# Gated delta stage: the decayed state enters the update banks by identity products, and ScalarE copies it back

## The reference, cut to what matters

```python
q = causal_dwconv_silu(x @ Wq.T, qcw, qcb).reshape(B, T, H, DK)
k = causal_dwconv_silu(x @ Wk.T, kcw, kcb).reshape(B, T, H, DK) * SCALE
v = causal_dwconv_silu(x @ Wv.T, vcw, vcb).reshape(B, T, H, DV)
a = sigmoid(x @ Wa.T + ba).reshape(B, T, H, DV)
beta = sigmoid(x @ Wb.T + bb)
def step(S, inp):                       # one token, all batches and heads
    qt, kt, vt, at, bt = inp
    err = einsum('bhij,bhj->bhi', S, kt) - vt
    S = at[..., None] * S - bt[..., None, None] * (err[..., None] * kt[:, :, None, :])
    return S, einsum('bhij,bhj->bhi', S, qt)
_, o = lax.scan(step, S0, xs)
o = (o - mean(o)) / sqrt(var(o) + EPS) * ln_w + ln_b      # over one head's 64 channels
o = (o * sigmoid(x @ Wg.T).reshape(B, T, H, DV)) @ Wo.T
```

## Time and profile before

| what | value |
| --- | --- |
| time before, median of 3 runs | 2882.89 us (2877.66 to 2885.38) |
| the profiled execution | 2865.99 us, span 2864.2 us |
| PE busy in the span | 2368.0 us, 83% |
| DVE busy in the span | 2144.6 us, 75% |
| ACT busy in the span | 1545.3 us, 54% |
| the gated delta stage | from about 53 to 1300 us of the span |

### The profile page before, as it was taken

One profiled execution on the slowest core, in us unless ns is written; L12 is line 12 of the kernel. 1 busy time (PEld: TensorE's weight loads), 2 busy tenths in 40 slices (PEclk: granted clock), 3 DMA queues, 4 the chain that ended last, 5 costly groups with the idle time before them and its releaser, 6 DMA issues. The chain is left out here.

```text
span 2864.2 us, 63246 instructions
## 1 busy us (share of the span) xinstructions
PE 2368.0 (83%) x25445; PEld 1633.2 (57%) x25445; DVE 2144.6 (75%) x4003; ACT 1545.3 (54%) x3976; POOL 264.0 (9%) x278
## 2 busy tenths in 40 slices
PE   6778778777777887787993999999997886999777
PEld 5677667666666777774441666666642232232376
DVE  6999999999999999993114677778726785886465
ACT  3555566666555555564233677777641113667344
POOL 0000000000000000000011101110002342110342
PEclk9788887888887787878996999999998998999889
DMA  5110111110111111102005999999500002230421
GB/s 184 32 31 18 31 31 32 32 32 17 31 32 32 32 24 24 31 17 71 1 11 151 230 248 227 237 240 233 137 32 11 0 1 86 59 98 24 170 71 64
DMA packets 205723, 219.44 MB, mean 77 GB/s; under 512 B 32966, under 2 KB 191446, under 8 KB 199990
## 3 DMA queue, kind: packets, MB, share of 16 engines
q1 hardware_dynamic: 203033, 210.44, 28.1%
q0 software_dynamic: 2400, 4.95, 0.5%
HBM read 137.96 MB, written 79.79 MB: 76 GB/s over the span
## 5 line engine op out<-in xcount | busy, mean ns | idle before, releaser
L2809 DVE TENSOR_REDUCE dl_ZO<-dl_XP 128x64 f32<-128x128 f32 (+6 forms) x448 | 219.7, 490 | 15.4
L2805 DVE TENSOR_TENSOR dl_XP<-dl_ZO,dl_G 128x64 f32<-128x64 f32 (+6 forms) x448 | 194.6, 434 | 15.4
L1990 ACT ACTIVATE da_AB<-ps 128x384 f32<-128x384 f32 x256 | 124.7, 491 | 142.4 <-PE ps L1851 138.7
L2143 DVE TENSOR_TENSOR ps<-ps,da_window 128x192 f32<-128x192 f32 (+1 forms) x256 | 101.3, 396 | 118.1 <-PE ps L1874 113.8
L1470 DVE TENSOR_REDUCE ra_top<-ps 128x1 f32<-128x512 f32 x256 | 159.2, 680 | 36.2 <-PE ps L1236 35.3
L2000 ACT ACTIVATE da_E<-ps,da_top 128x512 f32<-128x512 f32 x256 | 176.2, 688 | 17.4 <-DVE da_top L2146 16.9
L2146 DVE TENSOR_REDUCE da_top<-ps 128x1 f32<-128x512 f32 x256 | 176.9, 691 | 8.8
L1881 PE MATMUL ps<-ident,da_E 128*128 128x128 f32 x1024 | 168.8, 288 | 1.3 <-ACT da_E L2000 1.2
L1370 ACT ACTIVATE ra_PT<-ps 128x512 f32<-128x512 f32 x256 | 136.0, 601 | 61.0 <-PE ps L1267 60.7
L2380 PE MATMUL ps<-X,dl_taps_q 128*128 128x128 f32 x1088 | 149.7, 305 | 1.2 <-DVE dl_taps_q L2870 1.2
L2380 PEld LDWEIGHTS ps<-X,dl_taps_q 128*128 128x128 f32 x1088 | 146.5, 221 | 3.3 <-DVE dl_taps_q L2870 1.4
(11 more groups left out here) (408 smaller groups left out, 5760.5 us busy)
## 6 DMA issues: line engine op xcount, KB each, us to landing
da_bands<-da_AB SPq DMA_DIRECT2D x128, 384.0 KB, 3.8
dl_Abc<-dl_ends SPq DMA_DIRECT2D x64, 512.0 KB, 6.3
da_window<-da_bands SPq DMA_DIRECT2D x128, 192.0 KB, 4.3
da_across<-da_bands SPq DMA_DIRECT2D x128, 192.0 KB, 4.4
da_parts<-da_split SPq DMA_DIRECT2D x64, 96.0 KB, 3.4
ra_parts<-ra_split SPq DMA_DIRECT2D x16, 384.0 KB, 3.7
rf_We<-in_rf_We SPq DMA_DIRECT2D x1, 4608.0 KB, 23.3
da_K<-da_parts SPq DMA_DIRECT2D x16, 256.0 KB
```

The lines of the kernel that those rows point to most:

```text
L1990: eng.activation(AB[:, j % STAGES, h, :, :], ps[:, band_bank(v), 0:2 * BAND].rearrange("p (k x) -> p k x", k=2), ACT.Copy)\
L2805: link(eng.tensor_tensor(XP[:, :, :, SB - t:], seen.unsqueeze(1).to_broadcast([P, 2, I, t + 1]), G[:, x:x + 2, keys][:, ::-1, :].unsqueeze ...
L2809: link(eng.tensor_reduce(ZO[:, to:to + 1 + (2 * I - 1) * CH:CH].rearrange("p (k i) -> p k i", k=2), XP[:, :, :, SB - 1 - t:], AXX, ALU.add))
```

## The change

1. `end` on VectorE no longer adds. In `boundary` TensorE multiplies the identity with the decayed state's quarter into each update bank (`kept`), and the update products add to it. In the first half all four quarters are put in ahead of the wait for `W`; in the second half three, and the fourth comes after the updates of the first three, because its bank 1 is used for the transposes there. ScalarE copies each bank back to the state (`keep_state`), between the decays' copy (now `lay_decays`) and the rest of `lay_out`. VectorE waits for these copies before it decays the state again.
2. The transposes of `boundary` go to banks 2 and 3 in the first half and to bank 1 in the second, and the keys across to banks 2 and 3. TensorE's wait for the key copies moves behind the first two projections. The seventh projection moves ahead of the second `middle`.
3. The values are transposed into the buffer of the beta weights instead of `Y`, and `begin` waits only for the decays' copy.
4. In `steps` the first copy becomes a product with the second token's decay, and the first token's products read `XP` in place; the 32-element product of the second token is left out.
5. `norm` comes ahead of `prepare`, and its second product writes `Q` laid by row block, so that `out` reads contiguously.

```diff
+    TURNED = ((2, 3), (1, 1))
+    EARLY = (4, 3)
+    ACROSS = (2, 3)
-        values, decays = Y[:, 0:CH, :], Y[:, CH:, :]
+        values, decays = Wb[:, :, :].rearrange("p b x -> p (b x)").rearrange("p (t i) -> p t i", i=I), Y[:, CH:, :]
+        quarters = ST[:, :, :].rearrange("p (g r k) i -> p r g (k i)", r=GR, k=2)
...
+            def kept(r):
+                eng.matmul(ps[:, UPDATES[r], :], c.ident[:, :], quarters[:, r, :, :], start=True, stop=False)
+
+            def keep_early(n, e):
+                eng.wait_ge(s["decayed"], 2 * n + e + 1)
+                for r in range(EARLY[e]):
+                    kept(r)
...
-                for g in range(GR):
-                    for k in range(2):
-                        for h in range(2):
-                            for r in range(GR):
...
+                for g, k, h, r in itertools.product(range(GR), range(2), range(2), range(early)):
+                    update(g, k, h, r)
+                for r in range(early, GR):
+                    kept(r)
+                    for g, k, h in itertools.product(range(GR), range(2), range(2)):
+                        update(g, k, h, r)
...
-                Dv = D[:, :].rearrange("p (t m) -> p m t", m=M)
+                Dv = Q[:, :].rearrange("p (m x) -> p m x", m=M)
...
+                project(n + 1, 0, 2, True)
                 eng.wait_ge(s["ktc"], 5 * n + 5)
-                project(n + 1, 0, 2, True)
                 middle(n, 0)
...
+                keep_early(n, 0)
                 boundary(n, 0)
                 project(n + 1, AV, 6, True)
                 if not first:
                     out(n - 1)
+                project(n + 1, 6, 7, False)
                 middle(n, 1)
-                project(n + 1, 6, PROJ, False)
+                project(n + 1, 7, PROJ, False)
                 if not first:
                     eng.wait_ge(s["scaled"], n)
+                    eng.wait_ge(s["wo_copied"], n)
+                eng.wait_ge(s["evac"], (n + 1) * PROJ + 7)
+                keep_early(n, 1)
                 eng.wait_ge(s["begun"], BEGUN * (2 * n + 1) + 5)
                 products_of_keys(n + 1)
...
+            def keep_state(n, e):
+                for r in range(GR):
+                    eng.wait_ge(s["upd"], 8 * n + 4 * e + r + 1)
+                    eng.activation(quarters[:, r, :, :], ps[:, UPDATES[r], :].rearrange("p (g x) -> p g x", g=GR), ACT.Copy).then_inc(s["state"], 1)
...
                 boundary(n, 0)
+                lay_decays(n + 1, 0)
+                keep_state(n, 0)
                 lay_out(n + 1, 0)
...
-                eng.wait_ge(s["laid"], 4 * j)
+                eng.wait_ge(s["laid"], 4 * j - 3)
...
+                if j:
+                    eng.wait_ge(s["state"], 4 * j)
...
-                link(eng.tensor_copy(mine[:, :, 0], XP[:, 0, :, SB]))
+                link(eng.tensor_tensor(mine[:, :, 0], XP[:, 0, :, SB], aT[:, e, :, u, 2], ALU.mult))
                 for t in range(SB):
-                    if t:
+                    if t > 1:
...
-                eng.wait_ge(s["decayed"], j + 1)
-                quarters = ST[:, :, :].rearrange("p (g r k) i -> p r g (k i)", r=GR, k=2)
-                for r in range(GR):
-                    eng.wait_ge(s["upd"], 4 * j + r + 1)
-                    mine = quarters[:, r, :, :]
-                    eng.tensor_tensor(mine, mine, ps[:, UPDATES[r], :].rearrange("p (g x) -> p g x", g=GR), ALU.add).then_inc(s["state"], 1)
...
-                eng.scalar_tensor_tensor(D[:, :], D[:, :], vec[:, LB:LB + 1], gate[:, :, :].rearrange("p t n -> p (t n)"), ALU.add, ALU.mult)\
+                by_row = "p (x m) -> p x m"
+                eng.scalar_tensor_tensor(Q[:, :].rearrange("p (m x) -> p x m", m=M), D[:, :].rearrange(by_row, m=M), vec[:, LB:LB + 1],
+                                         gate[:, :, :].rearrange("p t n -> p (t n)").rearrange(by_row, m=M), ALU.add, ALU.mult)\
...
                 end(n, 0, first)
-                prepare(n + 1, 0)
                 if not first:
                     norm(n - 1)
+                prepare(n + 1, 0)
                 begin(n, 1)
```

More of the change, by code:

```diff
@@ L2430, in keys_across @@
                     for g in range(GR):
-                        mm = eng.transpose(ps[:, e, g * P:(g + 1) * P], kc[:, e, g * GP:(g + 1) * GP, :], c.ident[:, :])
+                        mm = eng.transpose(ps[:, ACROSS[e], g * P:(g + 1) * P], kc[:, e, g * GP:(g + 1) * GP, :], c.ident[:, :])
                     mm.then_inc(s["kt"], 1)
@@ L2448, in next_start, with update @@
                     start(1 - e, r)
+                def update(g, k, h, r):
+                    rows, cols = slice(32 * r, 32 * r + 32), slice(DK * h, DK * h + DK)
+                    at = (2 * g + k) * DK
+                    last = (g, k, h) == (GR - 1, 1, 1)
+                    mm = eng.matmul(ps[cols, UPDATES[r], at:at + DK], KT[rows, e, k, g, cols],
+                                    WT[rows, g, DK * (h ^ k):DK * (h ^ k) + DK], start=False, stop=(g, k) == (GR - 1, 1))
+                    if last:
+                        mm.then_inc(s["upd"], 1)
+                early = EARLY[e]
                 eng.wait_ge(s["w"], 4 * n + 2 * e + 2)
@@ L2453, in boundary @@
                     for g in (2 * half, 2 * half + 1):
-                        mm = eng.transpose(ps[:, half, (g % 2) * P:(g % 2 + 1) * P],
-                                           W[:, g * GP:(g + 1) * GP, :], c.ident[:, :])
+                        mm = eng.transpose(ps[:, TURNED[e][half], g * P:(g + 1) * P], W[:, g * GP:(g + 1) * GP, :], c.ident[:, :])
                     mm.then_inc(s["t"], 1)
@@ L2624, in boundary, with lay_decays @@
                 for half in range(2):
[L2625 to L2629, removed]
+                    eng.wait_ge(s["t"], 6 * n + 3 * e + (3 if e else half + 2))
+                    eng.activation(WT[:, 2 * half:2 * half + 2, :], ps[:, TURNED[e][half], half * 2 * P:(half + 1) * 2 * P].rearrange("p (g x) -> p g x", x=P),
+                                   ACT.Copy).then_inc(s["wc"], 1)
+            def lay_decays(m, e):
                 at = 2 * m + e + 1
@@ L2633, in lay_out @@
                    .then_inc(s["laid"], 1)
+            def keep_state(n, e):
+                for r in range(GR):
+                    eng.wait_ge(s["upd"], 8 * n + 4 * e + r + 1)
+                    eng.activation(quarters[:, r, :, :], ps[:, UPDATES[r], :].rearrange("p (g x) -> p g x", g=GR), ACT.Copy).then_inc(s["state"], 1)
+            def lay_out(m, e):
+                at = 2 * m + e + 1
                 for sign in range(2):
@@ L2673, in one_pass @@
                 boundary(n, 1)
+                lay_decays(n + 1, 1)
+                keep_state(n, 1)
                 lay_out(n + 1, 1)
@@ L2694, in _ @@
         def _(eng):
-            LINKS = 1 + 3 * SB - 1
+            LINKS = 3 * SB - 1
             def gate_keys(m):
@@ L2707, in turn_values @@
                 eng.wait_ge(s["evac"], m * PROJ + AV)
+                if 2 * m + e > 2:
+                    eng.wait_ge(s["laid"], 4 * (2 * m + e - 2))
                 eng.transpose(decays[:, :, :], aN[:, span, :]).then_inc(s["transposed"], 1)
@@ L2803, in steps @@
                     x, keys, seen = 2 * (at + t) + 1, slice(at, at + t + 1), mine[:, :, 0:t + 1]
-                    if t < SB - 1:
+                    if t == 0:
+                        link(eng.tensor_tensor(XP[:, ::-1, :, SB:], XP[:, 0, :, SB:].unsqueeze(1).to_broadcast([P, 2, I, 1]),
+                                               G[:, x:x + 2, keys].unsqueeze(2).to_broadcast([P, 2, I, 1]), ALU.mult))
+                    elif t < SB - 1:
                         link(eng.tensor_tensor(XP[:, :, :, SB - t:], seen.unsqueeze(1).to_broadcast([P, 2, I, t + 1]),
                                                G[:, x:x + 2, keys][:, ::-1, :].unsqueeze(2).to_broadcast([P, 2, I, t + 1]), ALU.mult))
+                    if t < SB - 1:
                         settled()
```

10 lines of the change are left out of this document (1 added, 9 removed).

## The result

The changed kernel is slower: 2895.25 us (median of 8 runs, the fastest 2886.77) against 2880.68 for the kernel before beside it (8 runs, 2876.93 to 2885.38). The ratio is 1.0045, 95% interval 1.0032 to 1.0057, so some 13 us more where 35 less were forecast. One of the 8 runs was disturbed (3615 us, granted clock 0.61), and the ratio leaves it out. The profiled execution took 2886.77 us, span 2885.0.

A forecast was written before the change was run, and what follows sets the result against it. VectorE was taken as the bound. 71.5 + 1.2 + 1.0 + 1.0 + 0.9 = 75.6 us a pass for 77.8, 35 us less over 16 passes: 2831 from the profiled 2866.0, 2848 as median; range 2806 to 2890.

The forecast's parts named there:

- VectorE alone: VectorE's pass without new waits: 77.8 us less additions, their wait and chain products, plus the stepped write, giving 71.5.
- The stepped write: Norm's second product on VectorE, writing with a step of 128 floats: 0.76 us on top of 1.285.
- Rival 4: Norm's stepped write costs as long again, 2.6 us: 9 us more in all, 2857; chance 0.06.
- The chains: Four step chains a pass on VectorE each lose a 32-element product of about 0.24 us: 0.96 us gone.
- (a): Middle of the first half: ScalarE late, VectorE waits 0.8 to 1.65 us a pass, 1.2 taken.
- (b): End of the first half: four identity products ahead of the transposes, wait 0 to 3.0 us, 1.0 taken.
- (c): Second middle: half of the q-projections ahead of it make TensorE late, 0.1 to 2.2 us, 1.0 taken.
- (d): End of the second half: no wait at full clock, 3.6 us at half clock after TensorE's gap; 0.9 taken.
- rival 3: Nothing left: waits add to 5.8 to 6.8 us a pass, 2874 to 2892 us; chance 0.10.
- rival 2: TensorE becomes the bound at 1.2 GHz, (b) with (c), and (d): slower by 27 us, 2910; chance 0.17.
- Rival 1: TensorE stays at 2.4 GHz: (b) and (d) vanish, 73.2 us a pass, -74 us, 2809; chance 0.20.

The follow-up runs named there:

- e5: Kernel before with only the step chains shortened (64 products of 32 elements left out); 2876.02 us against 2881.75, ratio 0.9977.
- e9: e8 with ScalarE's value copies of the second half moved behind the next pass's first evacuations; 2827.15 us against 2881.75, ratio 0.9813.
- e3: Changed kernel with two of the first half's four identity products ahead of TensorE's wait for the evacuated projections; 2867.91 us against 2882.12, ratio 0.9941.
- e2: Changed kernel with the seventh projection put back behind the second middle; 2848.25 us against 2882.12, ratio 0.9870.
- e12: e8 with norm's second product contiguous again and `out` reading with its step; 2819.22 us against 2865.96, ratio 0.9833.
- e8: Changed kernel with the edits of e2 and e3 together; 2830.23 us against 2881.75, ratio 0.9814.
- e4: Changed kernel without identity products, state copies and lone last quarter, VectorE adding as before; 2896.11 us against 2882.12, ratio 1.0049.
- e6: Kernel before with three unread identity products ahead of the first half's last transposes; 2872.46 us against 2865.96, ratio 1.0025.
- e1: Changed kernel with three unread identity products behind the products of keys, ahead of a pass's last transposes; 2878.34 us against 2882.12, ratio 0.9984.

## Why the prediction was wrong, point by point

**VectorE alone, 71.5 us: right.** 78.73 - 6.68 = 72.05 measured. The additions are gone. The stepped write was taken at 1.285 + 0.76 = 2.05 us:

```profile
L2870 DVE SCALAR_TENSOR_TENSOR dl_Q<-dl_D,dl_vec,dl_gate 128x1024 f32<-128x1024 f32 x15 | 30.4, 2028 | 0.5
```

0.73 ns an element for the step, as the stream transposes' pair in the earlier trace rows said. Rival 4 is out. The Trainium skill's Vector Engine (DVE) Microarchitecture Reference, section 5.2, has 2.50 ns a column for a destination that steps 24 words and 1.71 for one that hops 4 KiB, against 1.05 contiguous: 1.45 and 0.66 more. The 0.73 measured here for 128 words is near the second.

**The chains, 0.96 us: 0.4 or so.** The product that left stood between a reduction and the next product, which needs that reduction. After the change (VectorE, start and length):

```profile
601.36 0.31 DVE L2850 TENSOR_REDUCE dl_ZO<-dl_XP 128x64 f32<-128x128 f32 x1
601.70 0.30 DVE L2845 TENSOR_TENSOR dl_XP<-dl_ZO,dl_G 128x128 f32<-128x128 f32 x1
```

and before, where the small product lies in between:

```profile
600.67 0.30 DVE L2809 TENSOR_REDUCE dl_ZO<-dl_XP 128x64 f32<-128x128 f32 x1
600.89 0.21 DVE L2796 TENSOR_TENSOR dl_ZO<-dl_ZO,dl_aT 128x32 f32<-128x32 f32 x1
601.13 0.31 DVE L2805 TENSOR_TENSOR dl_XP<-dl_ZO,dl_G 128x128 f32<-128x128 f32 x1
```

From reduction to product 0.46 us became 0.34. The small product began 0.08 before the reduction's end, and the dependent one did not: half or more of the 0.24 was cover. With 0.09 (e5) to 0.12 (these rows) for each chain the term was 0.5 to 0.6 us a pass too large, about what the sum for VectorE alone missed.

**(a) 1.2 taken, 0.85 measured (0.91 over all passes): right in size and, in part, in kind.** ScalarE is late as said: in the changed kernel its copy for the middle stands right behind the gate, without idle time, 1.67 us behind the list, which is out at 609.93 (the sum had it 2.35 behind). In the kernel before it was 0.87 to 1.33 behind in all passes but the first.

```profile
609.85 1.98 ACT L2624 ACTIVATE dl_gate<-ps 128x128 f32<-128x128 f32 x8
611.60 0.65 ACT L2642 ACTIVATE dl_WT<-ps 128x512 f32<-128x512 f32 x1
```

What the sum did not have is the clock here: each half of the cross products took 1.12 us in this middle and 0.68 in the second, 0.9 us in all.

```profile
612.40 1.12 PE L2428 MATMUL ps<-dl_GX,dl_WT 64*64 64x64 f32 x16 [1.29 <-ACT dl_WT L2642]
...
650.59 0.68 PE L2428 MATMUL ps<-dl_GX,dl_WT 64*64 64x64 f32 x16 [0.78 <-ACT dl_WT L2642]
```

The four passes of e9 in which ScalarE was in time had slow cross products too and no wait, and with fast ones a copy at 1.67 would have been in time by the same rows (an estimate: 0.9 us earlier, for a wait of 0.85). So here it took both.

**(b) 1.0 taken, 1.54 measured (1.88 over all passes): right in kind**, inside 0 to 3.0. The identity products in front of the transposes took 3.70 us for 3.9, and e3 shows that they were on the path.

**(c) 1.0 taken, nothing in this pass.** The second middle was not held up (652.50, no bracket), and in all 16 passes together for 2.6 us. The moved half of the projections costs next to nothing where it went to; it costs where it came from, which the sum had under (d).

**(d) 0.9 taken, 4.29 measured: the step that failed.** The term's own working was nearly exact. It had VectorE ready at W+7.5: the begin would have started at 676.69 - 4.29 = 672.40, and W is 664.99, so W+7.4. It had the starts ready at W+6.8 at full clock, W+11.1 at half: measured W+11.7 in the changed kernel (676.69), and some W+7.1 in e2, at full clock. It even named the cause, "TensorE has now nothing for some 3.9 us ahead of W there, longer than the 2.82 after which the clock stood at 0.50"; the gap was 4.66. And then it took 0.9 of 3.6, a quarter, where its own row showed the lower clock after a shorter gap. It fell in 16 of 16 passes, and the term was 3.92 us a pass. With 3.6 in the sum the pass is 78.3 and the forecast 2891: rival 3's time, and just over the range's upper end of 2890. With the measured 4.29, 0.85, 1.54 and 0 instead of 4.1 in all, the waits are 6.68, past the 6.3 at which rival 2 breaks even.

**Rivals.** Rival 2 is what happened in its mechanism (TensorE at 1.2 GHz on the path) and its sign, with nearly all of it at one of its two places, (d), and 15 us instead of 27. Rival 1 (2.4 GHz kept) is what e2 gives for (d); with the old order the change takes 2848.25 us, the forecast's time, but by chance, since its waits are others. Rival 3 was the nearest in time (2874 to 2892).

**The other steps.** Both stood as said: ScalarE's state copies, and the output product, which had taken 3.89 us:

```profile
L2659 ACT ACTIVATE dl_ST<-ps 128x512 f32<-128x512 f32 x128 | 67.8, 601 | 53.1 <-PE ps L2466 53.0
```

```profile
643.85 1.95 PE L2517 MATMUL ps<-dl_Q,dl_Wo 128*128 128x128 f32 x16
```

The output product's 1.9 us less also lie ahead of the gap and may have widened it; that was not tried in the changed order. In the old order it does not look so: with the long output product (e12) the late identity product was slow in 5 passes of 16, with the short one (e8) in 1.

## What to carry to other kernels

When work is moved earlier on an in-order engine, cost the hole that it leaves as well as the delay that it makes: ask what runs right behind the hole, at which granted clock, and who waits for it. The same lower clock cost 7 us where the path behind it was short (e4) and 47 where it was long. If the trace shows a shorter gap after which the clock was halved, take the halved price as the value and not as the tail. A mean clock that rises says nothing: it was 0.87 after and 0.81 before, and what counts is the clock on the instructions that end the wait. And read in the trace whether an experiment did what it was to do, before its time is read: e9 left ScalarE late in 9 of 16 passes, and e6's fill ran into the work that it was to speed up.

## What the runs showed of the hardware

- The late path of some 270 small products took 11.4 us at a granted 0.50 and 7.1 at 1.00. In one kernel (e1) the clock held after an idle gap of 2.14 us in one pass and fell after one of 2.14 us in another, so the gap's length alone does not decide.
- In these chains a VectorE instruction that needs the one ahead starts about 0.03 us after its end (601.67 to 601.70), one that doesn't need it 0.08 before (600.89 for 600.97). Taking out such a one between two that hang together gave back 0.09 to 0.12 us of 0.24.
- A product of 128x1024 on VectorE that writes with a step of 128 floats took 2028 ns, the contiguous one 1285.
- The same late layer took 185.6 to 188.7 us in the four profiles from chips 1 and 2 and 202.0 to 205.4 in the eight from chips 4 and 9, whatever the kernel; the kernel before had a median of 2866 on chip 2 and 2882 on chips 4 and 9.
